# Attention probabilities transposed on VectorE in 32x32 blocks and by DMAs, in place of TensorE

## The reference, cut to what matters

```
q_h = cq @ W_qk[:, h]                     # 512 x 64
p_h = softmax(q_h @ ckv.T / 8)            # 512 x 1601
o_h = (p_h @ ckv) @ Wv_u[:, h]            # 512 x 64
x2  = layernorm(x1 + concat(o_h))
```

## Time and profile before

| | us |
|---|---|
| median of 3 runs (3110.32 to 3116.91) | 3111.46 |
| profiled execution | 3114.88 |
| its span, first to last instruction | 3112.8 |

### The profile page before, as it was taken

The page is one execution under the profiler, slowest core; times in us unless marked ns, Lnnn a source line. Parts: engine busy times, 40 slices in busy tenths (PEclk is TensorE's granted clock), DMA queues, the critical chain, the costliest instruction groups (busy, mean ns, idle before and its releaser), DMA issues. The chain is left out here.

```text
span 3112.8 us, 44510 instructions
## 1 busy us (share of the span) xinstructions
PE 2900.8 (93%) x16564; PEld 2292.3 (74%) x16564; DVE 2300.3 (74%) x2938; ACT 1577.5 (51%) x2543; POOL 1491.1 (48%) x728
## 2 busy tenths in 40 slices
PE   6776999999999999999999699999999699999997
PEld 3554677777777777777777478888887578888886
DVE  1526666766766676767776569999999689999998
ACT  2242555555655556555656354454543445454453
POOL 1000333301341034202430188888887488888884
PEclk8888999999999999999999799999999899999998
DMA  7305664401443044503350312222221322222221
GB/s 243 133 3 177 203 207 147 163 21 41 163 149 129 1 163 143 176 1 121 125 176 8 127 54 75 69 74 75 68 81 55 135 75 68 76 72 77 69 75 68
DMA packets 102198, 317.96 MB, mean 102 GB/s; under 512 B 11105, under 2 KB 30434, under 8 KB 101986
## 3 DMA queue, kind: packets, MB, share of 16 engines
q1 hardware_dynamic: 97122, 305.09, 28.7%
q10 hardware_dynamic: 4864, 10.03, 0.9%
HBM read 244.24 MB, written 70.85 MB: 101 GB/s over the span
## 5 line engine op out<-in xcount | busy, mean ns | idle before, releaser
L1101 DVE TENSOR_REDUCE b_mx<-b_sc 128x1 f32<-128x802 f32 (+1 forms) x512 | 483.8, 986 | 308.4 <-PE b_sc L850 305.7
L1407 DVE SCALAR_TENSOR_TENSOR c_acc<-c_ps,c_sd,c_acc 128x1024 f32<-128x1024 f32 x448 | 572.4, 1282 | 93.0 <-PE c_ps L1305 93.0
L1349 ACT ACTIVATE c_scaled<-c_ps,c_sgu 128x1024 f32<-128x1024 f32 x336 | 375.3, 1117 | 447.8 <-PE c_ps L1305 439.0
L983 ACT ACTIVATE b_pr<-b_sc,b_nm 128x802 f32<-128x802 f32 (+1 forms) x512 | 470.8, 925 | 177.5 <-DVE b_nm L1105 176.3
L1144 POOL TENSOR_TENSOR b_y<-b_y,b_yo 128x256 f32<-128x256 f32 x64 | 46.5, 727 | 970.0 <-DVE b_yo L1046 970.0
L1460 POOL TENSOR_TENSOR c_sum_u<-c_sum_u,c_scaled 128x1024 f32<-128x1024 f32 x168 | 404.7, 2409 | 78.9 <-ACT c_scaled L1349 77.9
L878 PE MATMUL b_po<-b_pt,shared 128*64 128x256 f32 x3328 | 442.0, 387 | 0.0
L1460 POOL TENSOR_TENSOR c_sum_g<-c_sum_g,c_scaled 128x1024 f32<-128x1024 f32 x168 | 404.8, 2410 | 67.2 <-ACT c_scaled L1349 66.6
L863 PE MATMUL b_tp<-ident,b_pr 128*128 128x128 f32 x3328 | 414.6, 274 | 0.7 <-DVE b_qs L1023 0.7
L850 PE MATMUL b_sc<-b_kh,b_qs 128*128 128x400 f32 (+1 forms) x1024 | 388.5, 379 | 20.5 <-ACT b_pr L983 16.4
L863 PEld LDWEIGHTS b_tp<-ident,b_pr 128*128 128x128 f32 x3328 | 379.7, 141 | 34.2 <-issue 9.3
(11 more groups left out here) (185 smaller groups left out, 4328.6 us busy)
## 6 DMA issues: line engine op xcount, KB each, us to landing
c_uw_int<-wint_u SPq DMA_DIRECT2D x56, 512.0 KB, 3.4
c_gw_int<-wint_g SPq DMA_DIRECT2D x56, 512.0 KB, 3.4
c_dw_int<-wint_d SPq DMA_DIRECT2D x56, 512.0 KB, 3.4
a_cx<-in_b_ctxT SPq DMA_DIRECT2D x16, 1608.0 KB, 11.1
b_rw<-in_c_gw SPq DMA_DIRECT2D x28, 512.0 KB, 3.8
b_rz<-in_c_gz SPq DMA_DIRECT2D x28, 512.0 KB, 4.8
b_rw<-in_c_uw SPq DMA_DIRECT2D x28, 512.0 KB, 4.0
b_rz<-in_c_uz SPq DMA_DIRECT2D x28, 512.0 KB, 5.4
```

What stands on the lines that cost most here:

```text
L983: S.activation(pr[q][:, k0:k1], sc[:, lo:hi], ACT.Exp, bias=nm[:, u % 2:u % 2 + 1], scale=0.125, accum_out=den[:, g % 2, q, half:half + 1] ...
L1101: V.tensor_reduce(mx[:, half:half + 1], sc[:, lo:hi], AX, ALU.max).then_inc(s_mb if half else s_ma, 1)
L1349: S.activation(dst[:, :], pair[SLOT[x, j] % 4][:, :], ACT.Identity, scale=scale(x, j)).then_inc(s_e, 1)
L1407: V.scalar_tensor_tensor(out=total, in0=pair[SLOT[x, j] % 4][:, :], scalar=scale(x, j), in1=total, op0=ALU.mult, op1=ALU.add).then_inc(s_a ...
```

## The change

- **Transposes.** The transposes on TensorE, the ring `tp` and the 7 copies of a pair go. VectorE turns each unit's probabilities in SBUF in place, 128 x 1632, in blocks of 32 x 32 (`V.transpose`). A row of `pr` is now seen as 4 quarters of 416 keys. SP then moves, for each pair, the 16 combinations of a partition quarter a and a column quarter c from `pr` to `pt` (`exchange`): partitions 32a to 32a+31 go to partitions 32c to 32c+31. Each of the 16 DMAs has 32 partitions x 2 units x 416 float32, in rows of 1664 bytes.
- **Keys.** After this, tile t holds keys 416c + 32t + i on partition 32c + i, so the tiles `cn` are made by 4 matmuls of 32 keys each in place of one transpose (`key_tile`).
- **Buffers.** `pr` has 6 rows in place of 4, `rz` 1 buffer in place of 2, and the second buffer of the keys goes. `sc` has 6 banks: the second half of a unit has one place, the first half two that alternate. `mi` is one bank for projections, outputs and key tiles.
- **Maximum.** One reduce takes both halves (2 x 802) and writes `nm`. The factor 1/8 is now in `cq`.
- **Order.** All queues run over a step k, one a unit. TensorE in step k: second half of the scores of unit k, projection, output, half of the `weigh` of pair (k-5)//2, then the first half of the scores of unit k+1. VectorE: maximum of k, transpose of k-1. ScalarE: exponential of the second half, then of the first.
- **GpSimd.** It takes the sums of a head over from VectorE and prepares one block a pair, in 21 pairs of each 32.
- **SP.** For each pair `exchange`, and in 84 pairs behind it `store(i)` and `load(i+1)`, so the loads run one block ahead in place of two. The rows of `y` are stored and loaded in pieces of 512 KB.

```diff
+def key_tile(kv, t, c):
+    return kv[0:LAT, c * (KPAD // 4) + 32 * t:c * (KPAD // 4) + 32 * t + 32]
...
-CN_AT = {(3, 2): (1, 0), (4, 2): (1, 1), (6, 2): (2, 0), (7, 2): (2, 1), (10, 2): (3, 0), (11, 2): (3, 1)}
+SEG = KPAD // 4
+TURNED = -(-NKV // 32) * 32
+SCORE = [[(0, 402, 110), (402, 400, 512)], [(798, 402, 110), (1200, 402, 512)]]
+SIDE = [(110, 912, 0, 802), (114, 913, 802, NKV)]
+CN_AT = {27: (1, 0), 35: (1, 1), 75: (2, 0), 83: (2, 1), 139: (3, 0), 147: (3, 1)}
+WEIGH_AT = 5
+OUT_AT = 10
+def block_of(p):
+    b, n = p // (PAIRS // L), p % (PAIRS // L)
+    return b * PER_BATCH + n if n < PER_BATCH else None
...
+        pr = sb("b_pr", [P, 6, 4, SEG])
+        pt = [sb(f"b_pt{j}", [P, 2, 4, SEG]) for j in range(2)]
...
+            def exchange(p):
+                s, u = p % 2, 2 * p % 6
+                Q.wait_ge(s_tt, 2 * p + 2)
+                if p >= 2:
+                    Q.wait_ge(s_pv, p - 1)
+                for shift in (2, 1, 3, 0):
+                    for a in range(4):
+                        c = (a + shift) % 4
+                        Q.dma_start(pt[s][32 * c:32 * c + 32, :, a, :], pr[32 * a:32 * a + 32, u:u + 2, c, :]).then_inc(s_move[s], 16)
+
             def load(i):
...
+                if i:
+                    Q.wait_ge(s_sub, i)
+                Q.dma_start(rz[:, :], raw[n + "z"][j:j + 1, :].broadcast_to([P, HID])).then_inc(s_rin[i % 2], 16)
...
+            for p in range(PAIRS):
+                exchange(p)
+                i = block_of(p)
+                if i is not None:
+                    store(i)
+                    if i + 1 < len(BLOCKS):
+                        load(i + 1)
...
             def scores(u, half):
...
+                if half and u:
+                    T.wait_ge(s_ex, 2 * u - 1)
+                elif u >= 2:
+                    T.wait_ge(s_ex, 2 * u - 2)
...
             def weigh(p, part):
                 if part == 0:
+                    moved(T, p)
...
+            for k in range(NU + OUT_AT):
+                if k < NU:
+                    scores(k, 1)
+                if k % 8 == 5 and k + 3 < NU:
+                    project((k + 3) // 4)
+                if k % 4 == OUT_AT % 4 and k >= OUT_AT:
+                    output((k - OUT_AT) // 4)
+                if k in CN_AT:
+                    turn_latent(*CN_AT[k])
+                if k >= WEIGH_AT and (k - WEIGH_AT) // 2 < PAIRS:
+                    weigh((k - WEIGH_AT) // 2, (k - WEIGH_AT) % 2)
+                if k + 1 < NU:
+                    scores(k + 1, 0)
...
+            def maximum(u):
+                first, second = half_at(u, 0) + SIDE[0][0], half_at(u, 1) + SIDE[1][0] - 3
+                V.wait_ge(s_sc, 2 * u + 2)
+                if u >= 2:
+                    V.wait_ge(s_ex, 2 * u - 2)
+                both = bass.AP(sc, min(first, second), [[3 * 1024, P], [abs(second - first), 2], [1, 802]])
+                V.tensor_reduce(nm[:, u % 2:u % 2 + 1], both, AXY, ALU.max, negate=True).then_inc(s_nm, 1)
+
+            def turn(u):
+                V.wait_ge(s_ex, 2 * u + 2)
+                V.transpose(row(u)[:, 0:TURNED], row(u)[:, 0:TURNED]).then_inc(s_tt, 1)
```

More of the change, by code:

```diff
@@ L324, in turn_keys @@
                 for t in CN_TURNS[k]:
-                    ins = T.transpose(ps[7][:, (t - CN_TURNS[k][0]) * LAT:(t - CN_TURNS[k][0] + 1) * LAT],
-                                      keys["kv"][0:LAT, t * P:(t + 1) * P], ident[0:LAT, 0:LAT])
+                    at = (t - CN_TURNS[k][0]) * LAT
+                    for c in range(4):
+                        ins = T.matmul(ps[7][32 * c:32 * c + 32, at:at + LAT], key_tile(keys["kv"], t, c), ident[0:LAT, 0:LAT],
+                                       start=True, stop=True)
                 ins.then_inc(s_cnp, 1)
@@ L666 @@
 PER_BATCH = len(BLOCKS) // L
[L667 to L672, removed]
+LN_SLOTS = [15, 16, 19, 20, 23, 24, 27, 28]
+LN_VAR, LN_FACTORS, LN_PAIR, STORE_PAIR = 31, 35, 20, 23
+WEIGH_AT = 5
[3 more added lines that the diff above has]
+    return b * PER_BATCH + n if n < PER_BATCH else None
 def ring_events():
     out = [("project", 0, 0)]
[L677 to L688, removed]
+    for k in range(NU + OUT_AT):
+        if k % 8 == 5 and k + 3 < NU:
+            out.append(("project", (k + 3) // 4, 0))
+        if k % 4 == OUT_AT % 4 and k >= OUT_AT:
+            out.append(("output", (k - OUT_AT) // 4, 0))
+        if k in CN_AT:
+            out.append(("cn", *CN_AT[k]))
     return out
@@ L818, in sync @@
+            for q in range(QT):
+                store_rows(L - 1, q)
             for k in range(2):
[L819 removed]
+                Q.wait_ge(stored[k], 16 * QT * L // 2)
                 Q.wait_ge(s_wout[k], 16 * len(BLOCKS) // 2)
@@ L828, in turn_latent @@
                 for t in chunk:
-                    ins = T.transpose(bank(ev)[:, (t - chunk[0]) * LAT:(t - chunk[0] + 1) * LAT],
-                                      kvs[b % 2][0:LAT, t * P:(t + 1) * P], ident[0:LAT, 0:LAT])
+                    at = (t - chunk[0]) * LAT
+                    for c in range(4):
+                        ins = T.matmul(mi[32 * c:32 * c + 32, at:at + LAT], key_tile(kv, t, c), ident[0:LAT, 0:LAT],
+                                       start=True, stop=True)
                 ins.then_inc(s_cnp, 1)
@@ L836, in project @@
                 b, h = g // HEADS, g % HEADS
-                T.matmul(bank(ev)[:, :], wqk[:, h:h + 2, :].rearrange("p a e -> p (a e)"), cq[:, b * NB:(b + 1) * NB],
+                T.matmul(mi[:, :], wqk[:, h:h + 2, :].rearrange("p a e -> p (a e)"), cq[:, b * NB:(b + 1) * NB],
                          start=True, stop=True).then_inc(s_q, 1)
[L840 to L852, removed]
@@ new lines, in tensor @@
+            scores(0, 0)
+            for k in range(NU + OUT_AT):
+                if k < NU:
+                    scores(k, 1)
+                if k % 8 == 5 and k + 3 < NU:
+                    project((k + 3) // 4)
+                if k % 4 == OUT_AT % 4 and k >= OUT_AT:
+                    output((k - OUT_AT) // 4)
+                if k in CN_AT:
+                    turn_latent(*CN_AT[k])
[3 more added lines that the diff above has]
+                    scores(k + 1, 0)
@@ L1159, in gpsimd @@
             split_keys(1)
-            for g in range(NHEAD):
-                if g:
-                    output(g - 1)
-                if g % HEADS == LN_AT + 4 and g > HEADS:
-                    normalise(g // HEADS - 1)
-                if g % HEADS == 1 and 1 <= g // HEADS <= 2:
-                    split_keys(g // HEADS + 1)
-                for i in heads_blocks(g):
-                    prepare(i)
-            output(NHEAD - 1)
+            for p in range(PAIRS + 4):
+                if p < PAIRS and block_of(p) is not None:
+                    prepare(block_of(p))
+                if p % 2 and p < PAIRS:
+                    sums(p // 2)
+                if p % 2 and p >= 5:
+                    output((p - 5) // 2)
+                b, n = p // (PAIRS // L), p % (PAIRS // L)
+                if 1 <= b < L and LN_PAIR <= n < LN_PAIR + QT:
+                    normalise(b - 1, n - LN_PAIR)
+                if n == 2 and 1 <= b <= 2:
+                    split_keys(b + 1)
         sync()
```

382 lines of the change are left out of this document (144 added, 238 removed).

## The result

The changed kernel takes 3344.6 us in the median (3338.2 to 3348.6, 4 runs), the kernel before 3112.4 beside it: 1.0744 times as long, 95% interval 1.0730 to 1.0757, so 232 us slower. I had forecast slower, by 118 us. The profiled execution has a span of 3343.7 us. Of the runs further down, one, of the kernel with 4 DMAs of 128 partitions, had TensorE's granted clock at 0.55 in the mean and took 4201 us; nothing is compared with it.

The account below looks back on a forecast made before the run. TensorE bounds the kernel before, SP's issuing the changed one: 84 x 11.8 + 44 x 10.3 = 1444 us, plus 24 at the ends, against 1336 + 14, adds 118 us: 3230 us, range 2930 to 3310.

Parts of the forecast that it names:

- the dear rows: Profile rows of DMA issues with few partitions or odd row lengths, used for SP's exchange: 0.65 us an issue with gap.
- Maximum, transpose: VectorE in attention: one maximum over 1604 columns 1.9 us, one transpose of 1632 columns 1.9 us.
- An exchange: SP's queue, each pair: issuing 16 DMAs one behind the other, 0.5 + 15 x 0.65 = 10.3 us.
- The block's three issues: SP's queue in 84 of 128 pairs: one store and two loads of a weight block, 3 x 0.47 = 1.4 us.
- The rows of y and the keys: SP's queue over the attention stage: some 40 further issues, about 20 us, left in the rounding.
- The sum: SP's queue over attention: 84 x 11.8 + 44 x 10.3 = 1444 us of exchanges; the stage grows by 118 us.
- Ports: Rival at the exchange's data: 32-partition DMAs run at 213 GB/s, 12.2 us with a block; 3227 or 3285 us; chance 0.24.
- the block's chain: Weight block's load, subtraction, cast and store follow each other: 9.9 us a block pair.
- The other side: Rival at SP's exchange: cheap issues, data at 376 GB/s; 2995 us (chance 0.24), or 2873 with block work hidden (0.06).
- TensorE's clock: Rival on TensorE: idling lowers its clock to 0.80, a pair takes 9.2 us, still hidden; only adds to slower cases.
- Load in turn: SP's loads run one block ahead, so load to store takes 9.9 us a block pair, hidden behind 10.3 of issues.
- The round trip: From one exchange's landing to the next-but-one's start: 19.6 us for two pairs, 9.8 a pair, just covered by issuing.

Follow-up runs that it names:

- without the diagonal: Against the changed kernel, the four blocks that stay on their partitions are copied by ScalarE and SP issues 12 DMAs: 3136.5 us, ratio 1.009.
- without the diagonal and with earlier loads: Against the kernel with four blocks copied by ScalarE, SP loads block i+1 mid-exchange and stores block i at its end: 3089.3 us, ratio 0.992.

## Why the prediction was wrong

The direction, the place and the mechanism were right: SP's issuing is the longest thing in a pair, an issue takes the 0.65 us that I took from the dear rows (now 0.60 + 0.04), TensorE's gain goes unused. The size was too small by half, and the time lies outside the range. The step that failed is the sum of SP's queue, and in it most of all the term for what stands between the exchanges. Step by step:

- **Maximum, transpose.** 1.9 and 1.9 forecast, 1.83 and 1.87 measured. Right. The loop between engines adds up to 4.03 us and not 4.1; nothing rested on it.
- **An exchange.** 10.3 us forecast, 10.26 where nothing stretches it, 10.59 in the mean, from its first issue to the end of its last. The 0.29 us of stretches and short waits, 38 us in all, were not in the sum.
- **The block's three issues.** This is the term that failed most: 3 x 0.47 = 1.4 us forecast, 2.05 measured (from 818.05, the end of an exchange, to 820.10). I had taken the rows of before, where such issues follow each other or stand alone. Behind an exchange the store takes 0.59 in place of 0.33. The broadcast of the zero points takes 0.79, and that is no work of the exchange: as the third of three in a row it takes as long in the kernel without one. The sum had 1.5 for the three: 10.25 + 1.41 is 11.66 and went in as 11.8, without which the forecast would have been 12 us lower still. The mean was 2.1, and 84 times 0.6 is 50 us.
- **The rows of y and the keys.** Left in the rounding, and forecast at about 20 us. 20 and 4 of their issues lie between the first exchange and the last, and take 17 us. Exchanges with nothing between them were 8 us apart in sum, 3 of them in one gap.
- **The sum.** From the first issue at 407.95 us to the end of the last at 1965.3 are 1557 us; forecast 1444. The terms above, 38, 50, 17 and 8, make the 113. The ends were right: the first exchange 15 us after the first scores, where I had 13, and the last add to y 8 us after the last issue, where I had 11. In a queue that never waits, every rounding is paid 128 times; I had a range for the 16 issues and none for what stands between them.
- **Ports.** I set them as a rival, to be chosen instead of the issues. They stand behind the first limit, together with the block's chain that they lengthen: the DMA engines are busy for 0.90 of a pair with a block, 11.2 us. Half the bytes gained 19 us, half the issues 168, a quarter of the issues with full partitions 305.
- **The other side.** Its condition, an issue under 0.59 us, was not met. Its 2995 us is near the 3040 of 4 DMAs, but not for its reason alone, since there the chain took 10.7 us and not 9.9.
- **TensorE's clock.** Forecast as a small addition. It fell to 0.89, and 14 weighings of 1.94 us take 3.67 behind an idle stretch. What it cost no run separates; SP waited for TensorE once, 0.8 us.
- **Load in turn.** Hidden in the changed kernel, as forecast (4 us of waits). It showed as soon as SP had fewer issues: 249 and 385 us of waits with 8 and 4 DMAs, 163 with 4 of 16 on ScalarE, 130 without the diagonal.
- **The round trip.** Forecast at 9.8 us, just covered. In the changed kernel it is, by the 19 us of waits for transposes. It shows where SP has fewer issues (90 us of waits without the diagonal and with earlier loads).

## What to carry to other kernels

When work goes from a compute engine to many small DMAs, add up the issuing queue first: number of DMAs times the issue time of a like DMA in a like place, with everything that stands between them, and give that sum a range of its own. Then set the bytes, at the rate of DMAs that reach as few partitions, beside it, not in its place: limits within a microsecond hide each other, and an edit that shortens only the first gives back no more than the distance to the next. Last, follow the chain of each buffer that is loaded and stored in turn in the same queue: its loads land later the fuller the DMA engines are, and it can be the next limit. A DMA issued from a second queue has to stand where that queue waits anyway and before the work that depends on its landing.

## What the runs showed of the hardware

- An issue of 32 partitions from SBUF to SBUF takes 0.60 us on SP's queue and 0.61 to 0.63 on ScalarE's (medians), at rows of 832, 1024 and 1664 B alike; both queues can issue at once. The first of four over 128 partitions takes 0.60 too.
- The mean of such issues is 0.62 us with 32 partitions in the changed kernel, 0.78 with 64 (DMA share 0.96) and 0.88 with 128 (0.82); single ones take up to 2.3.
- A store of 512 KB is issued in 0.33 us when SP stood idle before and in 0.59 directly behind such an exchange. The broadcast load of 512 KB takes 0.43 as the second of two issues and 0.79 as the third of three.
- DMAs of 64 partitions that alternate between the halves move 272 GB/s of busy share, DMAs of 128 partitions 350, both mixed with weight blocks.
- VectorE's 32x32 transpose in place of 128 x 1632 float32 takes 1.87 us, 1.15 ns a column; the tensor_tensor of 1024 columns takes 1.20.
- ScalarE copies 32 x 832 float32 from SBUF to SBUF in 0.88 us.
- The moving operand in pieces of 32 columns costs TensorE nothing: 14 weighings take 1.94 us at full clock, as before.
